# Rows and hidden rows of a top-2 expert layer turned by DMA transposes instead of on TensorE

## The reference, cut to what matters

```python
# x: (4, 512, 512), D = 512, 8 experts, hidden size H = 352, two experts for each token
x = x + softmax(ln(scaled sims of layernorm(x) and keys))         # attention part, 4 x 512 rows
n = layernorm(x)
scores = n @ Wg.T;  top 2 experts of each row, probs = softmax(top 2 scores)
for e in range(8):
    h = silu(n @ W1[e].T) * (n @ W2[e].T)                         # up products, 352 wide
    y = y + w[..., e:e+1] * (h @ W3[e].T)                         # down product, 512 wide
x = x + y
```

## Time and profile before

| | |
|---|---|
| median of 3 runs | 431.38 us (429.61 to 434.36) |
| the profiled execution's own time | 432.07 us |
| its span, first to last instruction | 430.3 us |
| PE busy | 354.9 us, 82% of the span |
| DVE, ACT, POOL busy | 273.9, 266.8, 212.2 us |
| mean granted PE clock | 0.887 of full speed |

### The profile page before, as it was taken

One profiled execution on the slowest core, in us unless ns is written; L12 is line 12 of the kernel. 1 busy time (PEld: TensorE's weight loads), 2 busy tenths in 40 slices (PEclk: granted clock), 3 DMA queues, 4 the chain that ended last, 5 costly groups with the idle time before them and its releaser, 6 DMA issues.

```text
span 430.3 us, 8658 instructions
## 1 busy us (share of the span) xinstructions
PE 354.9 (82%) x2023; PEld 230.2 (54%) x2024; DVE 273.9 (64%) x734; ACT 266.8 (62%) x458; POOL 212.2 (49%) x338
## 2 busy tenths in 40 slices
PE   2866489479486608899999999999999999999980
PEld 0432364365365505466666666666666666666640
DVE  1165767778798592666766766676676667667640
ACT  2378667767787491566666566666666656666640
POOL 1126536436456133355565565556556556655531
PEclk9998757868855558999999999999999999999995
DMA  7947564765656751134543544454454455445422
GB/s 236 418 194 232 221 214 159 289 208 163 220 192 211 230 222 51 50 61 89 95 70 80 98 75 77 93 94 66 85 98 74 76 94 86 72 87 94 79 34 40
DMA packets 21809, 57.28 MB, mean 133 GB/s; under 512 B 4832, under 2 KB 4960, under 8 KB 20256
## 3 DMA queue, kind: packets, MB, share of 16 engines
q0 software_dynamic: 8736, 20.53, 27.4%
q1 hardware_dynamic: 13056, 36.56, 24.8%
HBM read 38.17 MB, written 18.91 MB: 133 GB/s over the span
## 4 chain that ended last, share of the span: by engine, by line
PE 55%; DVE 4%; DMA 3%; issue 1%; POOL 1%; POOLq 0%; ACT 0%; DVEq 0%; ACTq 0%
PE bank L1072 31%; PE bank L1102 17%; PE bank L1063 4%; PE bank L1087 3%; DMA x_s<-n_table,gcol 2%; DVE stage L840 2%; DMA out<-kvj_s,scol 1%; POOLq L65 0%; POOL w3rs L485 0%; PE bank L1040 0%; DVE stage L836 0%; POOL gcol L468 0%; DVEq L890 0%; DVE kvg_s L882 0%; ACT kvj_s L631 0%
## 5 line engine op out<-in xcount | busy, mean ns | idle before, releaser
L873 DVE SCALAR_TENSOR_TENSOR stage<-W,w3sc,stage 128x512 f16<-128x512 f16 x117 | 84.1, 746 | 6.8 <-ACT stage L604 6.8
L1102 PE MATMUL bank<-stage,n_s 128*128 128x512 f16 (+1 forms) x351 | 82.2, 379 | 1.5 <-issue 1.5
L604 ACT ACTIVATE stage<-W,w3sc 128x512 f16 x117 | 79.5, 717 | 0.0
L1072 PE MATMUL bank<-Wp,kvg_s 128*128 x480 | 78.0, 312 | 0.2 <-issue 0.2
L1072 PE MATMUL bank<-Wp,kv_s 128*128 x456 | 74.2, 312 | 0.0
L1072 PEld LDWEIGHTS bank<-Wp,kvg_s 128*128 128x128 f16 x480 | 46.7, 97 | 25.8 <-issue 4.1
L901 DVE TENSOR_TENSOR n_s<-bank,n_s 128x384 f16<-128x384 f32 x39 | 21.7, 557 | 59.7 <-ACT n_s L620 59.7
L1072 PEld LDWEIGHTS bank<-Wp,kv_s 128*128 128x128 f16 x456 | 44.5, 98 | 24.2
L470 POOL DMA_INDIRECT x_s<-n_table,gcol x39 | 50.4, 1293 | 6.8 <-issue 5.1
L1102 PEld LDWEIGHTS bank<-stage,n_s 128*128 128x128 f16 (+1 forms) x351 | 34.2, 98 | 34.5 <-issue 1.7
L616 ACT ACTIVATE L_s<-bank,winv 128x352 f32<-128x352 f32 x39 | 21.6, 553 | 45.0 <-PE bank L1072 41.4
(11 more groups left out here) (161 smaller groups left out, 586.1 us busy)
## 6 DMA issues: line engine op xcount, KB each, us to landing
W<-in_w SPq DMA_DIRECT2D x8, 1408.0 KB, 7.3
W<-in_w SPq DMA_DIRECT2D x8, 768.0 KB, 5.9
stage<-in_xT SPq DMA_DIRECT2D x4, 1024.0 KB, 6.5
x_s<-in_x SPq DMA_DIRECT2D x16, 256.0 KB, 6.2
out<-x_s SPq DMA_DIRECT2D x16, 256.0 KB, 4.3
n_table<-n_s SPq DMA_DIRECT2D x16, 256.0 KB, 2.7
stage<-in_ctxT SPq DMA_DIRECT2D x1, 768.0 KB, 8.2
x_s<-n_table,gcol POOLq DMA_INDIRECT x39
```

Of the source, the lines that this page charges most:

```text
L604: eng.activation(w3p[r][:, c * D:(c + 1) * D], W3[:, bass.ds(e * W3N + c * D, D)], ACT.Copy, scale=w3sc[:, bass.ds(e, 1)]).then_inc(s_w3h, 1)
L873: eng.scalar_tensor_tensor(w3p[r][:, W3N + c * D:W3N + (c + 1) * D], W3[:, bass.ds(e * W3N + c * D, D)], w3sc[:, bass.ds(e, 1)], w3p[r][:, ...
L1072: mm = eng.matmul(bank[2 * which + r][:, 0:H], n_, w_, start=(c == 0 and k == 0), stop=(c == DC - 1 and k == 2))
L1102: mm = eng.matmul(bank[4 if r else 7][:, :], h_, w_, start=(c == 0 and k == 0), stop=(c == HC - 1 and k == 2))
```

## The change

Gathered rows are no longer turned on PE, nor is `hid`. Four things replace it:

1. In the attention part ACT writes the high fp16 half of each normalised row times 1024, and DVE the low half, into a new tile `row_s`. SP stores `row_s` as the row of the table, one slot later than it stored `n_s`. The bytes of a row stay the same.
2. In the expert part SP turns the gathered fp16 pairs with one DMA transpose for each tile (128 rows x 1024 fp16, `turn_rows`), straight into `nTm`. ACT and DVE write the two halves of `hid` side by side into `h16` (zeros beyond column 352), and SP turns these by a second DMA transpose (128 x 768 fp16) into `hT`.
3. There are three buffers for gathered rows, `nTm` and `hT` instead of two. POOL issues the gather of tile t+3, then the scatter of tile t, taking the index columns directly, without a copy.
4. PE's order in tile t is: both up products of t, then the down product of t-2. The W3 split on ACT and DVE moves one tile later too. All tile bodies are written out, without the hardware loop. The descriptor scratch of the POOL queue is set to 8192 bytes.

```diff
-        ng = [x_flat[:, k * ROW:(k + 1) * ROW] for k in range(2)]
-        nTm = [v[:, :].bitcast(F16) for v in (kvg_s, kv_s)]
+        ng = [x_flat[:, k * ROW:(k + 1) * ROW] for k in range(3)]
+        ng16 = [v.bitcast(F16)[:, 0:2 * D] for v in ng]
+        nTm = [v[:, :].bitcast(F16) for v in (kvg_s, kv_s, prod_s)]
...
@@ sync
+            def turn_rows(t):
+                if t >= NT:
+                    return
+                eng.wait_ge(s_ng[t % 3], 16 * (t // 3 + 1))
+                wait(eng, s_bp, t - 2)
+                eng.dma_start_transpose(nTm[t % 3].rearrange("p (c m) -> p c m", m=P), ng16[t % 3]).then_inc(s_nt[t % 3], 16)
+
+            for t in range(3):
+                turn_rows(t)
+            eng.wait_ge(s_hp, 2)
+            for t in range(NT):
+                eng.wait_ge(s_hl, t + 1)
+                wait(eng, s_yp, t - 2)
+                eng.dma_start_transpose(hT[t % 3].rearrange("p k (c m) -> p (k c) m", m=P), h16[t % 2]).then_inc(s_hd[t % 3], 16)
+                turn_rows(t + 3)
...
@@ gpsimd
-                eng.tensor_copy(gcol[:, r:r + 1], gidx[:, bass.ds(t, 1)]).then_inc(s_gc, 1)
-                hold(eng, 1, (s_gc, t + 1))
-                eng.indirect_dma_start(out=ng[r], out_offset=None, in_=n_table,
-                                       in_offset=bass.IndirectOffsetOnAxis(ap=gcol[:, r:r + 1], axis=0)).then_inc(s_ng[r], 16)
+                wait(eng, s_nt[t % 3], 16 * (t // 3))
+                wait(eng, s_wm, t - 2)
+                eng.indirect_dma_start(out=ng[t % 3], out_offset=None, in_=n_table,
+                                       in_offset=bass.IndirectOffsetOnAxis(ap=gidx[:, t:t + 1], axis=0)).then_inc(s_ng[t % 3], 16)
+
+            for t in range(3):
+                gather(t)
...
+            for t in range(NT):
+                gather(t + 3)
+                eng.wait_ge(s_y, t + 1)
+                wait(eng, s_sct, 16 * t)
+                eng.indirect_dma_start(out=out, out_offset=bass.IndirectOffsetOnAxis(ap=sidx[:, t:t + 1], axis=0),
+                                       in_=ym[t % 2], in_offset=None, compute_op=ALU.add).then_inc(s_sct, 16)
...
@@ scalar
+                b2, i2 = lag(b, i, 2)
+                if real(b2):
+                    g, k = g_of(b2, i2), i2 % 2
+                    eng.wait_ge(s_n, g + 1)
+                    wait(eng, s_stn[k], 16 * (g // 2))
+                    eng.activation(row_s[:, k, 0:D], n_s[:, k, :], ACT.Copy, scale=NSCALE).then_inc(s_rh, 1)
...
-                    eng.activation(nTm[r][:, 0:D], bank[5][:, :], ACT.Copy, scale=NSCALE).then_inc(s_mT, 1)
-                    eng.activation(hT[1 - r][:, 0, :], bank[6][:, 0:HC * P], ACT.Copy).then_inc(s_hT, 1)
+                    eng.activation(h16[r][:, 0:H], hid[r], ACT.Copy).then_inc(s_hh, 1)
...
+                if t >= 2:
+                    eng.wait_ge(s_yp, t - 1)
+                    eng.wait_ge(s_wm, t - 1)
+                    wait(eng, s_sct, 16 * (t - 3))
+                    eng.activation(ym[r], ybank(t)[:, :], ACT.Copy, scale=wm[:, (t - 2) % 4:(t - 2) % 4 + 1]).then_inc(s_y, 1)
...
@@ vector
+                    eng.wait_ge(s_rh, g + 1)
+                    eng.scalar_tensor_tensor(row_s[:, k, D:2 * D], n_s[:, k, :], NSCALE, row_s[:, k, 0:D], ALU.mult,
+                                             ALU.subtract).then_inc(s_rl, 1)
...
+                    eng.wait_ge(s_hh, t + 1)
+                    eng.tensor_tensor(h16[r][:, HC * P:HC * P + H], hid[r], h16[r][:, 0:H], ALU.subtract).then_inc(s_hl, 1)
...
@@ tensor
-                for c in range(DC):
-                    mm = eng.transpose(bank[5][:, c * P:(c + 1) * P], ng[r][:, c * P:(c + 1) * P], ident[:, :])
-                mm.then_inc(s_mTp, 1)
...
+            def tile(t):
+                r = t % 2
+                if t < NT:
+                    e = eng.value_load(ecoli[0:1, t:t + 1], min_val=0, max_val=E - 1)
+                    eng.wait_ge(s_nt[t % 3], 16 * (t // 3 + 1))
+                    wait(eng, s_a, t - 1)
+                    up(e, 0, t).then_inc(s_ap, 1)
+                if t < NT:
+                    wait(eng, s_h, t - 1)
+                    up(e, 1, t).then_inc(s_bp, 1)
+                if t >= 2:
+                    eng.wait_ge(s_w3l, HC * (t - 1))
+                    eng.wait_ge(s_hd[(t - 2) % 3], 16 * ((t - 2) // 3 + 1))
+                    wait(eng, s_y, t - 3)
...
-    nc = bacc.Bacc("TRN2", target_bir_lowering=False, num_devices=1)
+    nc = bacc.Bacc("TRN2", target_bir_lowering=False, num_devices=1, dynamic_dma_scratch_size=8192)
```

More of the change, by code:

```diff
@@ L231, in build @@
         s_idx = sem("s_idx")
[L233 to L236, removed]
+        s_ng = [sem(f"s_ng{i}") for i in range(3)]
+        s_nt = [sem(f"s_nt{i}") for i in range(3)]
+        s_hd = [sem(f"s_hd{i}") for i in range(3)]
+        s_ap, s_a, s_bp, s_h, s_hp, s_hh, s_hl, s_yp, s_y, s_ws, s_wm = [
+            sem(n) for n in ("s_ap", "s_a", "s_bp", "s_h", "s_hp", "s_hh", "s_hl", "s_yp", "s_y", "s_ws", "s_wm")]
+        s_sct = sem("s_sct")
         NCONST = 15
@@ L279, in g_of, with ybank @@
             return b * TPB + i
[L282 to L298, removed]
+        def ybank(t):
+            return bank[7] if t % 2 else bank[4]
         block = ctx.enter_context(nc.Block())
@@ L616, in tile @@
                     eng.activation(act_a[r], bank[r][:, 0:H], ACT.Silu, scale=winv[:, bass.ds(e, 1)]).then_inc(s_a, 1)
-                if exists(t - 1):
-                    eng.wait_ge(s_hTp, t)
-                    wait(eng, s_yp, t - 2)
-                    eng.activation(hT[1 - r][:, 0, :], bank[6][:, 0:HC * P], ACT.Copy).then_inc(s_hT, 1)
[L621 to L631, removed]
+                if 0 <= t - 1 < NT:
+                    w3_high(t - 1, e_last, 0)
+                    w3_high(t - 1, e_last, 1)
+                if t < NT:
+                    eng.wait_ge(s_h, t + 1)
+                    if t >= 2:
+                        eng.wait_ge(s_hd[(t - 2) % 3], 16 * ((t - 2) // 3 + 1))
+                    eng.activation(h16[r][:, 0:H], hid[r], ACT.Copy).then_inc(s_hh, 1)
+                if 0 <= t - 1 < NT:
+                    w3_high(t - 1, e_last, 2)
+                if t >= 2:
[3 more added lines that the diff above has]
+                    eng.activation(ym[r], ybank(t)[:, :], ACT.Copy, scale=wm[:, (t - 2) % 4:(t - 2) % 4 + 1]).then_inc(s_y, 1)
+                return e
             eng.wait_ge(s_et, 1)
-            eng.wait_ge(s_tab, 1)
             eng.wait_ge(s_winv, 2 * E)
-            mT_evac(0, 0)
-            mT_evac(0, 1)
             eng.wait_ge(s_w3sc, 1)
-            expert_tiles(eng, tile)
+            e = None
+            for t in range(NT + 2):
+                e = tile(t, e)
         @block.vector
@@ L874, in w3_low, with tile @@
                                          w3sc[:, bass.ds(e, 1)], w3p[r][:, c * D:(c + 1) * D], ALU.mult, ALU.subtract).then_inc(s_w3l, 1)
[L876 to L886, removed]
+            def tile(t, e_last):
+                r = t % 2
@@ L905, in tile @@
                     eng.wait_ge(s_bp, t + 1)
-                    wait(eng, s_hTp, t - 1)
+                    wait(eng, s_hl, t - 1)
                     eng.scalar_tensor_tensor(hid[r], bank[2 + r][:, 0:H], winvh[:, bass.ds(e, 1)], act_a[r], ALU.mult, ALU.mult).then_inc(s_h, 1)
[L908 to L911, removed]
+                if 0 <= t - 1 < NT:
+                    w3_low(t - 1, e_last, 1)
@@ L912, in _ @@
+                if t < NT:
+                    eng.wait_ge(s_hh, t + 1)
+                    eng.tensor_tensor(h16[r][:, HC * P:HC * P + H], hid[r], h16[r][:, 0:H], ALU.subtract).then_inc(s_hl, 1)
+                if 0 <= t - 1 < NT:
+                    w3_low(t - 1, e_last, 2)
+                return e
             eng.wait_ge(s_et, 1)
-            low_rows(0, 0)
-            low_rows(0, 1)
+            for r in range(2):
+                eng.memset(h16[r].rearrange("p (k m) -> p k m", k=2)[:, :, H:HC * P], 0.0).then_inc(s_hp, 1)
@@ L915, in _ @@
             w3_scale()
             eng.wait_ge(s_yinv, 1)
-            expert_tiles(eng, tile)
+            e = None
+            for t in range(NT + 1):
+                e = tile(t, e)
         @block.tensor
@@ L1052, in _, with up @@
             warm(oh[:, :, :, :].rearrange("p g k e -> p (g k e)"), WARM_GATHER)
-            def turn_rows(j, r):
-                if not exists(2 * j + r):
-                    return
-                t = 2 * j + r
-                eng.wait_ge(s_ng[r], 16 * (j + 1))
-                wait(eng, s_mT, t)
-                wait(eng, s_ml, t)
-                for c in range(DC):
-                    mm = eng.transpose(bank[5][:, c * P:(c + 1) * P], ng[r][:, c * P:(c + 1) * P], ident[:, :])
-                mm.then_inc(s_mTp, 1)
-            def up(e, which, r):
-                for c in range(DC):
-                    n_high, n_low = [nTm[r][:, k * D + c * P:k * D + (c + 1) * P] for k in range(2)]
+            def up(e, which, t):
```

(11 more changed lines are left out.)

116 lines of the change are left out of this document (41 added, 75 removed).

## The result

The changed kernel takes 578.62 us (median of 4 runs, 577.05 to 581.64), against 432.87 us before (4 runs): 1.339 times as long, with an interval of 1.328 to 1.349. The prediction was 551 us, with a range of 478 to 680.

A forecast was written before the change was run, and what follows sets the result against it. PE alone was taken to bound the kernel before, a gather-behind-scatter loop the changed one. 432.1 us + 108 (expert part) + 8 (attention) + 1 (start) + 3 (end) = 552; median 551 us, range 478 to 680.

The forecast's parts named there:

- the step on POOL: POOL's in-order queue: gather t+3 waits behind scatter t-1; 6.8 us plus the rows' DMA transpose where 5.5 are free.
- The sum of the loop: Expert part: two PE turns take 6.8 + 4.6 + 7.17 = 18.6 us, a tile 9.3 against 6.29, +108 us.
- X: DMA transpose of the gathered rows, issued by SP once the gather has landed: 4.6 us, ends 2.7 and 13.6.
- the pieces: Short source pieces of a DMA transpose: 1024 for the rows, 768 for `h16`, priced from the store of `wrow`.
- The second transpose: SP's DMA transpose of `h16`, queued behind the rows': 3.45 us, just hidden behind the up products' 3.58 us.
- the clock: PE's granted clock falls while PE waits: 0.77 taken, ends 0.65 and 1, making 5.52 us of PE work 7.17.
- The attention part: 16 added fp32-to-fp16 copies on ACT and 16 on DVE, partly on the path: +8 us, ends 0 and 23.
- start and end: First rows turned by DMA, +1 us; copies and DMA transpose before the last down product, +3 us.
- A: Rival: transposes are hidden and PE stays the bound at 5.52 us a tile, 414 us; chance 3%.
- B: Rival: DMA pieces are dear, rows' transpose 13.6 us and `h16` 10.2, a tile 16.3, some 815 us; chance 13%.
- C: Rival: rows' transpose costs a plain transfer's 2.7 us, gaps too short for the clock to fall, 485 us; chance 22%.
- D: Rival: descriptor scratch too small, so the gather starts only when the scatter has landed; +1.6 us a tile, 608 us; 5%.

The follow-up runs named there:

- The first two experiments: Changed kernel with only the gather moved earlier in POOL's queue: gather t+4 ahead of scatter t, 458.66 us; then gather t+5 ahead, 443.18 us.
- gather five ahead: Changed kernel with gather t+5, in place of t+3, ahead of scatter t on POOL, three buffers as before: 443.18 us.

## Why the prediction was right

**What bounds, and the step on POOL.** Right, and shown: the gather behind the late scatter made a loop of two turns. The first two experiments opened it by order alone, for 120 and 135 us.

**The sum of the loop.** 18.6 us were forecast for two turns; 20.6 were measured, in the mean and in the turns shown. By terms, in the turns shown: result rows 0.8, measured 0.73; to the scatter 0.86, measured 0.46 (no instruction to hold the wait); scatter to gather 1.6, measured 1.91; gather 3.5, measured 4.3 there and 6.3 in the other path (382.86 to 389.17), behind a scatter and beside transposes; X 4.6, measured 5.1 from issue to PE's start; PE 7.17, measured 8.1. The two that were sized too low by most are the gather, priced by a row in which no scatter ran ahead of it, and PE: the mean clock was 0.81, near the 0.77 taken, but the half clock falls on the up products behind the wait, all of which are in the loop, and not on PE's work evenly.

**X and the pieces.** The size of X was right, and that was in part luck. 4.6 was the estimate for a transpose alone, 13.6 for one beside other transfers. In the changed kernel one with no scatter or gather beside it landed 3.1 to 3.8 us after its issue, mostly 3.2 or 3.3. The one of each two that is on the path, beside a scatter and a gather, took 4.4 to 7.3, mostly 4.6 to 5.2 (for `prod_s` the profile has no landing). So the price per piece, taken from `wrow`, was too high in both cases, and the lower of its two results happened to fit the crowded case. The pieces themselves are there, as the page's line on the hardware queue says (packets first):

```profile
q1 hardware_dynamic: 85440, 54.46, 35.6%
```

Before, it was 13056, so 1856 more for each tile, against 1024 and 768 forecast. The hidden rows' transpose took 2.7 to 2.9 us with no scatter or gather beside it, against 3.45, and 5.2 to 6.2 with them. Doubling X moved the time by about half of it, as the sum says.

The Trainium skill (Advanced Engine Details and Errata, X-Bar Transpose) says that transposing DMAs are as fast as ordinary ones. With no scatter or gather beside them the trace comes near to it: 3.2 us, against 2.7 for the plain store of the same 256 KB to device memory. The crowded case, 4.4 to 7.3 us, was the one that counted here. The Trainium skill's 1309 ns for a block (VectorE: DVE Perf Modes, The three transpose paths) would make 10.5 us for eight blocks in series, as an estimate. They don't add up like that: eight blocks took 3.1 to 7.3 us.

**The second transpose, and the clock.** Hidden, as forecast: leaving it out gained nothing. The granted clock falls in such a wait as the one shown, and the up products behind it take 6.0 us in place of 3.6, which is 1.2 us a tile. Keeping PE busy took 43.5 us off, but it set a pace of its own and spaced the turns evenly, so it doesn't price the clock. (The fall that the prediction reads at 114.6 us lies nearer 114.3 by its row, 0.63 in that us; nothing rests on it.)

**The attention part, start and end.** For the attention part 8 us were forecast, 6.4 are in the trace and 7.0 in the run with the copies. With the first rows' turn it was to be 9, and the first down product does come 8.8 us later. The end was to cost 3 us more and took 3.4 less: from the 37th down product to the end of the span it is 19.8 us, where it was 23.2.

**The rivals.** A (hidden transposes) needed the gather not to wait for the scatter; when that was arranged, the DMA engines filled and the scatters came late, which the rival did not have. B had X too high; C had it too low for a transpose beside other transfers, and the gaps, 7 us at every second tile, were no short ones. D is excluded: the gather started 1.91 us behind the scatter, which landed 4.8 us after its issue.

The sum ended 28 us below the measured time. The loop was sized 1.0 us a tile too low, 36 us in all, and the end 6 us too high.

## What to carry to other kernels

When a product is moved later, follow its result into every in-order queue: here it was not the transposes but a gather standing behind the scatter of that result that cost 120 us, and one line's order gave them back. Count the short pieces of a new DMA (the count was borne out here, the price of a piece was not), and check what the DMA engines' busy share will be once the waits are gone, and how late it makes transfers that wait for each other, as the scatters do here; moving a transpose off PE paid only for the one beside which the scatters landed as fast as before. A wait that comes back each turn also costs the clock, on the very work behind it.

## What the runs showed of the hardware

A DMA transpose of 128 x 1024 fp16 from SBUF to SBUF landed 3.1 to 3.8 us after its issue with no scatter or gather beside it and in 4.4 to 7.3 us with them; it held SP for 1.23 us. One of 128 x 768 took 2.7 to 2.9 us and 5.2 to 6.2. A tile's two made some 1850 packets. Both in each tile, with a gather and a scatter of 256 KB, filled the DMA engines (share 1.00, gather five ahead, 220 to 300 us) while only 156 GB/s were moved. An accumulating scatter of 256 KB landed in 4.8 us before the change and in 4.7 to 4.8 beside the hidden rows' transpose, and took 5.6 with both transposes; scatters that wait for each other started 6.6 us apart then.
